# Linear-attention block in fp32: the last quarter of the keys is projected before the second quarter of the queries, and VectorE follows that order

## The reference, cut to what matters

```
q, k, v = x @ Wq.T + bq, x @ Wk.T + bk, x @ Wv.T + bv      # split into 16 heads of 16
q = softmax(q, axis=-1)                                    # over the 16 channels of a head
k = softmax(k, axis=-2)                                    # over the 1024 tokens
state = einsum('bhnd,bhne->bhde', k, v)
out = einsum('bhnd,bhde->bhne', q, state)
out = layer_norm(out) @ Wo.T + bo
x = layer_norm(x + out)
```

## Time and profile before

| | before |
|---|---|
| median of 3 runs | 551.4 us (551.26 to 551.43) |
| the profiled execution | 551.22 us, span of its instructions 549.3 us |
| TensorE matmul busy | 532.3 us (97%) |
| VectorE busy | 482.0 us (88%) |
| ScalarE busy | 479.1 us (87%) |
| GpSimd busy | 415.0 us (76%) |
| granted TensorE clock, mean | 0.996 of full speed |

### The profile page before, as it was taken

The page is one execution under the profiler, slowest core; times in us unless marked ns, Lnnn a source line. Parts: engine busy times, 40 slices in busy tenths (PEclk is TensorE's granted clock), DMA queues, the critical chain, the costliest instruction groups (busy, mean ns, idle before and its releaser), DMA issues.

```text
span 549.3 us, 10912 instructions
## 1 busy us (share of the span) xinstructions
PE 532.3 (97%) x3541; PEld 492.4 (90%) x3541; DVE 482.0 (88%) x1227; ACT 479.1 (87%) x952; POOL 415.0 (76%) x429
## 2 busy tenths in 40 slices
PE   8999999999999999989999999999999999999993
PEld 7999999898999989879987999999999999999992
DVE  6878998989899898878788899999999999999896
ACT  5836799798979878778799999999999999999996
POOL 3965979877796986478468878888888877776782
PEclk9999999999999999999999999999999999999998
DMA  8620050320705021070011003322125253010002
GB/s 335 223 105 1 1 231 2 147 84 29 280 1 230 2 100 56 1 268 3 0 40 41 1 0 117 117 77 80 53 63 116 77 94 95 34 52 38 39 39 116
DMA packets 12679, 46.51 MB, mean 85 GB/s; under 512 B 1360, under 2 KB 3792, under 8 KB 10448
## 3 DMA queue, kind: packets, MB, share of 16 engines
q1 hardware_dynamic: 12336, 45.28, 24.1%
q10 hardware_dynamic: 288, 0.54, 0.3%
HBM read 29.01 MB, written 16.81 MB: 83 GB/s over the span
## 4 chain that ended last, share of the span: by engine, by line
PE 68%; ACT 11%; DVE 11%; POOL 5%; issue 3%; DMA 1%; POOLq 0%; DVEq 0%; ACTq 0%
PE qps_sps_aps_then_y L2029 19%; PE ring L2007 19%; PE qps_sps_aps_then_y L1789 6%; PE qps_sps_aps_then_y L1895 5%; PE qps_sps_aps_then_y L1875 5%; PE ring L1817 5%; DVE z L1287 3%; PE ring L1947 2%; POOL xt_lo L464 2%; PE ring L1922 1%; PE ring L1910 1%; ACT ek L747 1%; PE ring L1962 1%; POOL ff_accp_over_xt_lo L590 1%; POOL xt L475 1%
## 5 line engine op out<-in xcount | busy, mean ns | idle before, releaser
L2029 PE MATMUL qps_sps_aps_then_y<-ff_w_over_xc_lo,ff_a_lo_over_qw 128*128 128x258 f32 x512 | 126.5, 283 | 0.0
L2029 PE MATMUL qps_sps_aps_then_y<-ff_w_over_xc_lo,ff_a_hi_over_xc_lo 128*128 128x258 f32 x512 | 126.4, 283 | 0.0
L1369 DVE SCALAR_TENSOR_TENSOR ff_a_lo_over_qw<-ring,ff_rho,ff_a_hi_over_xc_lo 128x512 fp32r<-128x512 f32 x128 | 92.9, 744 | 12.5 <-ACT ff_a_hi_over_xc_lo L883 11.1
L2007 PE MATMUL ring<-ff_ht_hi_over_qw,t 128*128 128x512 f32 x256 | 103.7, 405 | 0.2
L2007 PE MATMUL ring<-ff_ht_lo_over_xc_hi,t 128*128 128x512 f32 x256 | 100.5, 392 | 0.0
L2029 PEld LDWEIGHTS qps_sps_aps_then_y<-ff_w_over_xc_lo,ff_a_hi_over_xc_lo 128*128 128x128 f32 x512 | 96.7, 189 | 3.4
L2029 PEld LDWEIGHTS qps_sps_aps_then_y<-ff_w_over_xc_lo,ff_a_lo_over_qw 128*128 128x128 f32 x512 | 96.8, 189 | 3.3
L865 ACT ACTIVATE ring<-ring,bias 128x512 f32<-128x512 f32 x128 | 84.8, 691 | 6.5 <-PE ring L2007 3.7
L590 POOL TENSOR_TENSOR ff_accp_over_xt_lo<-ff_accp_over_xt_lo,ff_sq_over_ek_et_hi 128x512 f32<-128x512 f32 x66 | 86.0, 1304 | 2.0
L881 ACT ACTIVATE ff_sq_over_ek_et_hi<-ring 128x512 f32<-128x512 f32 x128 | 80.6, 630 | 0.5
L883 ACT CAST ff_a_hi_over_xc_lo<-ring 128x512 fp32r<-128x512 f32 x128 | 79.5, 621 | 0.0
(11 more groups left out here) (200 smaller groups left out, 1616.7 us busy)
## 6 DMA issues: line engine op xcount, KB each, us to landing
xt<-in_x_tok_dram SPq DMA_DIRECT2D x8, 1024.0 KB, 4.8
out_dram<-ff_z_over_et_lo SPq DMA_DIRECT2D x15, 512.0 KB, 3.3
x_scratch<-z SPq DMA_DIRECT2D x14, 514.0 KB, 3.5
ff_x_over_w_raw_xc<-x_scratch SPq DMA_DIRECT2D x14, 514.0 KB, 5.2
xc<-in_x_chan_dram SPq DMA_DIRECT2D x6, 1024.0 KB, 6.9
w_raw<-in_w_dram SPq DMA_DIRECT2D x2, 1024.0 KB, 5.6
ek<-in_x_chan_dram SPq DMA_DIRECT2D x1, 1024.0 KB, 8.0
x_scratch<-xt SPq DMA_DIRECT2D x2, 512.0 KB, 8.3
```

Source lines behind the costliest of these rows:

```text
L1369: nc.vector.scalar_tensor_tensor(out=ff_a_lo[:, m % DEPTH], in0=ff_bank(k, m), scalar=ff_rho[:, m:m + 1], in1=ff_a_hi[:, m % DEPTH].bitcas ...
L2007: mm = nc.tensor.matmul(ff_bank(k, m), t1[:, c, m * P:(m + 1) * P], h[:, k % 2, c], start=(c == 0 and j == 0), stop=(c == CH - 1 and j == 1))
L2029: last = nc.tensor.matmul(ff_yps[:, t, 0:C + 2], a[:, m % DEPTH, t * P:(t + 1) * P], ff_w2[:, m], start=(m == 0 and j == 0), stop=(m == FC ...
```

## The change

In the loop over b = 1 to 6, TensorE computes the last quarter of the keys right behind `state_project`, and the second quarter of the queries after it (before: the other way round). VectorE's list is put into the same order: `q_maximum(b + 1, 1)` goes behind `k_maximum(b, 1)`, `q_centre(b + 1, 1)` directly behind it, and `q_inverse(b, 1)` behind both. No instruction is added or removed; the lists of ScalarE, GpSimd and SyncE are as they were.

```
@@ VectorE, loop over b
                 k_maximum(b, 0)
                 projected(b - 1)
                 q_centre(b + 1, 0)
-                q_maximum(b + 1, 1)
                 projected_low(b - 1)
                 k_maximum(b, 1)
+                q_maximum(b + 1, 1)
+                q_centre(b + 1, 1)
                 q_inverse(b, 1)
-                q_centre(b + 1, 1)
                 q_maximum(b + 1, 2)
                 product_stats(b - 1, 0)
                 q_centre(b + 1, 2)
@@ TensorE, loop over b
                 state_transpose(b - 1)
                 k_product(b, 1, 0)
                 state_project(b - 1)
+                k_product(b, 1, 1)
                 q_product(b + 1, 1)
-                k_product(b, 1, 1)
                 q_product(b + 1, 2)
                 attend(b - 1, 0)
```

## The result

The change makes the kernel slower: 556.84 us, the median of four executions (556.56 to 558.28), against 551.41 of four executions of the kernel before (551.26 to 551.43). The ratio is 1.0103, with a 95% interval of 1.0092 to 1.0115, so **5.4 us more**.

The account below looks back on a forecast made before the run. TensorE was taken as barely the bound, paced by a loop over GpSimd and VectorE. Terms: 5.65 - 0.42 + 1.0 = 6.2 us on the 551.4 us median, forecast 557.6 us, range 553.4 to 559.3 us.

Parts of the forecast that it names:

- The loop over GpSimd and VectorE: Attention passes: GpSimd from `q_normalise` to `rsA`, VectorE from residual to reciprocal; 32.51 us a turn against TensorE's 31.4 us.
- 5 x 1.13 us: Second reciprocal comes 1.13 us later, paid anew in five turns from pass 1 to 6: 5.65 us.
- `projected_low` 0.20 us earlier, not 0.60: VectorE, pass 3: without the query maximum ahead, it still waits for `r_hi`, so it starts only 0.20 us earlier.
- 3.23 + 0.60: VectorE: from `projected_low` 3.23 us to the second centre's start, then 0.60 us to the second reciprocal.
- 0.42 us of slack: Pass 4: VectorE's waits for TensorE, 0.26 and 0.16 us, absorb lateness in one turn; 0.42 us off.
- The shared read, 1.0 us: GpSimd's `tok_c` overlapping VectorE's residual: four turns gain the overlap one had, 0.25 us each, 1.0 us in all.
- TensorE's swap costs nothing: TensorE's two swapped blocks: no matmul added, query quarter ends before its maximum's new place, covered by VectorE's list; cost nothing.
- The centre, at most 0.12 us in a pass: Second `q_centre` on VectorE ends 0.12 us later, TensorE's fourth query quarter follows; does not add up, taken as 0.
- rival 4: Later `q_normalise` holds up third query transpose or state sum, a microsecond more in four turns: 561.6 us; chance 0.02.
- Rival 1: TensorE's waits for ScalarE ahead of `state_sum` in passes 3 and 6 absorb part: 552.8 to 555.8 us; chance 0.17.
- Rivals 2 and 3: No difference, GpSimd's share shortens, 551.4 to 551.8 us, chance 0.08; faster, shorter way to `r_lo`, 550.2 us, chance 0.07.
- What was to show it: Second `q_normalise` of pass 2 to pass 3's 33.6 us instead of 32.51; more TensorE idle before L1842 or L1764.

Follow-up runs that it names:

- e9: Kernel before, with the second reciprocal moved directly behind `projected_low`, ahead of the key maximum: 549.22 us.
- e3: Changed kernel with the second reciprocal put back right behind the key maximum, ahead of the second query maximum and centre: 551.72 us.
- e5: Kernel before, with only the second reciprocal and second query centre swapped, so the reciprocal comes one step later: 554.12 us.
- e2: Kernel before with VectorE's new list alone, TensorE's blocks left in their old order: 556.98 us.
- e7: Changed kernel with the second reciprocal three steps later still, behind the centre of the third query quarter: 566.80 us.
- e1: Kernel before with TensorE's two blocks swapped alone, VectorE's list as it was: 557.10 us.
- e6: Kernel before, with the second reciprocal moved ahead of the second query maximum, `projected_low` and the keys: 554.33 us.
- e8: Kernel before with TensorE's blocks swapped and, on VectorE, only the second reciprocal moved, ahead of the second query maximum: 558.02 us.
- e10: Kernel before with TensorE's blocks swapped and, on VectorE, only the second reciprocal moved, directly behind `projected_low`: 554.82 us.
- e11: Changed kernel with the second reciprocal ahead of `projected_low`, and ScalarE's two ternary writes of passes 3 and 6 three steps later: 547.68 us.

## Why the prediction was right

The forecast (557.6 us, slower) holds, by its main mechanism. Point by point:

- **The loop over GpSimd and VectorE.** Shown. The reciprocal was placed at five points of VectorE's list with little else changed: ahead of the keys (e9) 549.2 us, behind them (before, e3) 551.3 and 551.7, behind the centre too (e5) 554.1, behind maximum and centre (the change, e2) 556.8 and 557.0, three steps further (e7) 566.8. Every step later costs about its own length five times, less in e7 (the clock apart, 7.1 for 8.2 us); the earlier place gives back 2.0 us, after which TensorE has no wait left at L1842 to lose.
- **5 x 1.13 us.** Forecast 5.65. The second `q_normalise` shows 167.84 - 161.06 = 6.78 us over the five turns; take off the 1.05 us that VectorE waited for the slow L1850, and 5.73 us stay. The turns are not alike: 1.10, 1.04, 1.32, 0.93 and 1.34 us. In e2 they are 1.14, 1.09, 1.11, 0.93 and 1.33, together 5.60.
- **`projected_low` 0.20 us earlier, not 0.60.** Right: 1.77 instead of 1.98 us behind `projected`, with the wait for `r_hi` that was foreseen. The reciprocal follows it by 3.83 us, the forecast's 3.23 + 0.60.
- **0.42 us of slack.** The two waits of pass 4 are gone, as forecast, but the turn that held them grew by 1.32 us, not by 1.13 - 0.42 = 0.71. What took the gain back is a shared read that the forecast did not have, in another place. In pass 4 `projected_low` takes 1.86 us instead of 0.95, because GpSimd's first `q_normalise` is under way:

```profile
145.02 1.95 POOL L485 TENSOR_TENSOR qw<-qw,qinv 128x1024 f32<-128x1024 f32 x1
...
145.92 1.86 DVE L1146 TENSOR_TENSOR r_lo<-r_f,r_hi 128x768 fp32r<-128x768 f32 x1 [0.30 <-ACT r_hi L790]
```

  In e2 the same instruction takes 1.41 us, and the turn grows by 1.11. The passes on TensorE grew by 6.8 - 1.6 = 5.2 us, which equals 5.65 - 0.42; with the turns at 5.6 to 5.7, that equality is no proof of the term, and where TensorE saves the difference was not traced.
- **The shared read, 1.0 us: the term that failed.** `tok_c` at the ends of passes 1 to 5 takes 2.46, 2.47, 2.40, 2.46 and 2.46 us, against 2.41, 2.67, 2.42, 2.41 and 2.40 before. Summed up, that is 0.06 us less, not 1.0 more. I priced the overlap at GpSimd, and there it is 0.05 us. I also took it for something that only one turn had; the kernel before has it at all five ends of passes, one residual instruction of 2.41, 2.62, 1.66, 2.45 and 2.66 us each. Two of these rows, the first of them right behind the row of 0.45 us that I read:

```profile
96.94 2.62 DVE L1287 SCALAR_TENSOR_TENSOR z<-z,rsA,xt 128x256 f32<-128x256 f32 x1
...
161.41 2.45 DVE L1287 SCALAR_TENSOR_TENSOR z<-z,rsA,xt 128x256 f32<-128x256 f32 x1
```

  So the bound of one VectorE instruction, 0.45 us, holds only where VectorE is first. Where GpSimd is first it is VectorE's residual that pays, in the changed kernel too, as the timeline shows where pass 2 begins:

```profile
65.93 2.61 DVE L1287 SCALAR_TENSOR_TENSOR z<-z,rsA,xt 128x256 f32<-128x256 f32 x1
...
69.86 0.49 DVE L1287 SCALAR_TENSOR_TENSOR z<-z,rsA,xt 128x256 f32<-128x256 f32 x1 [0.30 <-POOL rsA L497]
```

  The first of these takes 2.61 us, through GpSimd's `tok_c` (65.79, 2.46 us), and the second, without it, 0.49. It costs nothing, since VectorE still waits 0.30 us for `rsA` behind it. Without this term the sum would have given 551.4 + 5.2 = 556.6 us, against 556.8. That this is so near is in part luck: the 0.42 us taken off and the 0.91 us of `projected_low` in pass 4 are both in the measured time, and only the first is in the sum.
- **TensorE's swap costs nothing.** Right in the change and wrong by itself. e2 and the whole change are equal; e1 costs 5.9 us. The cover that the forecast named, VectorE's list, is what carries it.
- **The centre, at most 0.12 us in a pass.** Small, as said: L1764 waits once, for 0.33 us. Next to it stands something not foreseen, 0.39 and 0.31 us at L1910, the query transposes, for ScalarE's key exponential. This is not rival 4, which has GpSimd's `q_normalise` as the releaser and 4 us as its price; here it is ScalarE and 0.7 us.
- **Rival 1** (ScalarE's waits cover part) has fallen: the 1.8 us at L1895 are as large after as before, so ScalarE moves with the loop. Rivals 2 and 3 have fallen: the kernel is slower, clear of noise.
- **What was to show it.** The distance from pass 2's to pass 3's second `q_normalise` was to be 33.6 us and is 34.60, of which 1.05 is the slow clock. L1842 waits more in passes 3 and 6 and newly in 5; in 4 it is L1764, 0.33 us, and in 2 the wait at L1910, which was not named. The idle time in passes 2, 4 and 5 is less than they grew by (the busy time of their windows grew as well, 31.44 to 32.01 us in pass 2), so part of their growth stands in no row of waits.
- **Not foreseen: the clock.** The longer wait brought a fall of the clock in one of the four executions (mean granted clock 0.993, the others 0.995). One execution of e2 is alike, 558.09 us at 0.992, without a trace. It is outside the sum, and moves no median here; in e7 it does.

## What to carry to other kernels

An engine that is 97% busy can still be paced by a loop over two others: add up the two legs between two handovers that follow each other without a pause, and compare with what the busy engine needs. In such a loop, a short instruction that releases the other engine belongs ahead of everything that nobody waits for, and each microsecond of delay is paid once in every turn. But look at what the release starts: moved too early (e6, e8), it set a long GpSimd instruction running across a VectorE one that TensorE waited for, and the gain became a loss.

## What the runs showed of the hardware

**VectorE and GpSimd locking each other out.** A VectorE instruction with two SBUF inputs takes 2.51 or 1.86 us instead of 0.95 (`projected_low`), or 2.61 instead of 0.49 (residual), when a GpSimd `tensor_tensor` over 1024 columns is under way. `projected_low` ends 0.81 us behind GpSimd's instruction in both cases (e6: 112.89 and 112.08; the changed kernel: 147.78 and 146.97), so it does most of its work when the other is done. When VectorE's begins first, it takes 1.03 us and GpSimd's pair takes 4.55 instead of 3.96 us. The Trainium skill, "SBUF — State Buffer", section "Who interferes with whom", says that a VectorE instruction with two SBUF inputs contends with a GpSimd one that reads SBUF, that the lock is exclusive, and that the order of issue decides who blocks. These rows agree, and they show what my sum did not use of it: the price depends on which of the two is late.

**The clock can fall after a short idle time, and its length alone does not decide.** TensorE fell to 1.2 GHz after 1.83 us (in one of four executions), 2.05 and 3.41 us of idle time, and stayed at 2.4 GHz after 1.79 us, after 1.81 us (e2, pass 3) and after 2.93 us. The one fall in the trace of the changed kernel cost TensorE 1.6 us. What else decides it stays open; no run was made for it.

Also open: how the remaining 3.6 us of e10 divide over the short way in a pass, why the passes grow by 5.2 us where the loop's turns grow by 5.6 to 5.7, and why e11's one wait of 1.0 us for GpSimd's `q_normalise` appears. None of them bears on which step causes the change's 5.4 us.
